# A graph-attention kernel: the attention stage with segmented maxima on 56 partitions, PSUM operands for VectorE, and an unrolled order

## What is computed

```
feat_src = (feat @ W_n).reshape(N, H, D)
el, er = einsum('nhd,hdt->nht', feat_src, attn_l / attn_r);  em = einsum('ef,hft->eht', e_pro, attn_m)
e = (einsum(el[src], mask) + einsum(er[dst], mask) + einsum(em, mask)) / 3.0
e = where(e > 0, e, NEG_SLOPE * e)
e_max = segment_max(e, dst)
e_exp = exp(e - e_max[dst])
a = e_exp / segment_sum(e_exp, dst)[dst]
rst = segment_sum(feat_src[src] * a[:, :, None], dst)
...
x = x + attention(relu(layernorm(x)));  x = x + layers(relu(layernorm(x)))
```

## Time and profile before

| what | us |
|---|---|
| median of 3 runs | 4303.44 |
| lowest, highest | 4292.51, 4304.95 |
| the profiled execution, its own time | 4305.03 |
| its span in the profile | 4301.5 |
| gathers of the attention stage: first start | 155.1 |
| last weighing of rows (L1506) starts | 1680.7 |

### The profile page before, as it was taken

One profiled execution on the slowest core, in us unless ns is written; L12 is line 12 of the kernel. 1 busy time (PEld: TensorE's weight loads), 2 busy tenths in 40 slices (PEclk: granted clock), 3 DMA queues, 4 the chain that ended last, 5 costly groups with the idle time before them and its releaser, 6 DMA issues.

```text
span 4301.5 us, 47883 instructions
## 1 busy us (share of the span) xinstructions
PE 3329.9 (77%) x13132; PEld 2370.4 (55%) x13132; DVE 2106.5 (49%) x5235; ACT 1030.1 (24%) x2694; POOL 3076.5 (72%) x2940
## 2 busy tenths in 40 slices
PE   4378888777877777888888868888887687878765
PEld 3266666555555564555666545565665455555554
DVE  4588888666666676222332422233333223344354
ACT  2134444333333343111111210111112111111111
POOL 0368878687878784777777757777777577777775
PEclk9678888777677788999999988999999889999987
DMA  4367777544444454665666436666664366666653
GB/s 150 106 176 217 220 217 222 167 131 133 130 134 135 133 162 120 196 192 185 190 188 193 141 117 193 185 197 189 195 186 138 112 201 193 197 197 210 190 147 111
DMA packets 441679, 730.92 MB, mean 170 GB/s; under 512 B 113602, under 2 KB 290894, under 8 KB 441390
## 3 DMA queue, kind: packets, MB, share of 16 engines
q0 software_dynamic: 139888, 388.79, 32.5%
q1 hardware_dynamic: 299436, 336.87, 24.3%
q10 hardware_dynamic: 2066, 1.93, 0.1%
HBM read 608.13 MB, written 119.14 MB: 169 GB/s over the span
## 4 chain that ended last, share of the span: by engine, by line
POOL 37%; issue 12%; PE 8%; DMA 3%; DVE 0%; ACT 0%; SPq 0%; POOLq 0%; DVEq 0%
POOL ring L457 37%; PE ps L1176 4%; PE ps L1124 2%; DMA block_sums<-message_sums 1%; DMA ring<-message_table,src_index 1%; PE ps L1160 1%; PE ps L1153 1%; PE ps L1193 1%; DMA message_sums<-sums_out 0%; PE ps L585 0%; DMA message_table<-block_msg 0%; DVE block_cube L691 0%; DVE block_inv_norm L693 0%; SPq L1055 0%; DVE block_o L1230 0%
## 5 line engine op out<-in xcount | busy, mean ns | idle before, releaser
L457 POOL DMA_INDIRECT ring<-message_table,src_index x1995 | 1888.1, 946 | 716.0 <-issue 603.8
L1176 PE MATMUL ps<-ring,one_hot 128*128 128x256 f32 x3990 | 1089.2, 426 | 361.3 <-DMA ring<-message_table,src_index 354.0
L457 POOL DMA_INDIRECT ring<-attention_table,src_index x784 | 1023.2, 1305 | 294.0 <-issue 236.8
L1176 PEld LDWEIGHTS ps<-ring,one_hot 128*128 128x128 f32 x3990 | 829.2, 214 | 651.2 <-DMA ring<-message_table,src_index 467.4
L1230 DVE SCALAR_TENSOR_TENSOR block_o<-ps,inv_deg,root 128x256 f32<-128x256 f32 x147 | 71.0, 483 | 1013.1 <-PE ps L1153 1013.0
L1124 PE MATMUL ps<-attention_work 128*128 128x512 f32 x1176 | 550.8, 600 | 20.3 <-DMA attention_work<-message_table 20.3
L521 PE MATMUL ps<-ring,one_hot 128*128 128x265 f32 x1568 | 531.2, 478 | 8.9 <-issue 7.5
L521 PEld LDWEIGHTS ps<-ring,one_hot 128*128 128x128 f32 x1568 | 337.8, 233 | 96.2 <-issue 33.0
L1124 PEld LDWEIGHTS ps<-attention_work 128*128 128x128 f32 x1176 | 226.7, 193 | 240.2 <-issue 205.0
L1210 DVE TENSOR_SCALAR shift_mat<-ps,shift_by 128x128 f32<-128x128 f32 x282 | 97.5, 346 | 490.0 <-PE ps L1193 445.9
L1273 ACT ACTIVATE sums_out<-ps 128x256 f32<-128x256 f32 x285 | 109.1, 383 | 865.6 <-PE ps L1193 810.7
(11 more groups left out here) (157 smaller groups left out, 3666.3 us busy)
## 6 DMA issues: line engine op xcount, KB each, us to landing
attention_work<-dense_adjacency SPq DMA_DIRECT2D x294, 256.0 KB, 3.0
attention_work<-in_dst_edges SPq DMA_DIRECT2D x112, 448.0 KB
attention_work<-message_table SPq DMA_DIRECT2D x294, 128.0 KB, 3.6
message_sums<-sums_out SPq DMA_DIRECT2D x285, 128.0 KB, 2.2
ring<-message_table,src_index POOLq DMA_INDIRECT x1995
dense_adjacency<-root SPq DMA_DIRECT2D x49, 512.0 KB
message_table<-block_msg SPq DMA_DIRECT2D x147, 128.0 KB, 2.7
block_sums<-message_sums SPq DMA_DIRECT2D x123, 128.0 KB, 3.5
```

What stands on the lines that cost most here:

```text
L457: pool.indirect_dma_start(m.ring[:, k, t, 0:cols], None, table, bass.IndirectOffsetOnAxis(ap=m.src[:, at:at + 1], axis=0)).then_inc(s[f"ro ...
L1176: last = nc.tensor.matmul(m.ps[:, 6 + parity, 0:D], m.one_hot[:, parity, t, :], m.ring[:, k, t, 0:D], start=(t == 0), stop=(only and t == ...
```

## The change

`attention` is written anew.

- Maxima are taken inside a tile of 128 edges with a halo of 48 edges at each side (RUN goes from 40 to 48), so the 7 tiles x 8 heads lie on 56 partitions, each 224 long (REACH). A check in `setup` covers all edges and sends a graph with a run longer than that to the general path. With full maxima the running rescale (`drop`, `fall`, `carry`) is gone.
- Each large VectorE operation has one operand in PSUM: the weights that ACT writes, the forward scan, and the constants of the comparisons.
- PE adds the gathered left scores to the kinds with an identity matmul. The one-hot matrices are made by DVE with one comparison instead of by ACT.
- The inverse square root of the node step is computed on DVE.
- All engines' programs are unrolled, and the order of steps is another.

The diff, cut to its core:

```diff
-RUN = 40
+RUN = 48
+REACH = P + 2 * RUN
 @block.tensor
+            def left_of(c):
+                rows_in(pe, c)
+                nc.tensor.matmul(m.ps[:, 0, 0:TILES * 32].rearrange("p (t n) -> p t n", t=TILES), m.ident[:],
+                                 m.ring[:, c % SLOTS, :, WIDE:ROW], start=False, stop=True).then_inc(s["kinds"].sem, 1)
+            def to_heads(c):
+                if c + 1 < CHUNKS:
+                    pe.wait_ge(s["leaky"].sem, s["leaky"].done(c + 1))
...
+                nc.tensor.matmul(m.ps[0:cols, 1, RUN:RUN + P], m.score[:, at:at + cols], m.ident[:], start=True, stop=True)
...
+            def to_edges(c):
+                cols = TILES * HEADS
+                pe.wait_ge(s["bwd"].sem, s["bwd"].done(c))
+                nc.tensor.transpose(m.ps[:, 1, 512 - cols:512], m.seg_max, m.ident[0:cols, 0:cols]).then_inc(s["mt"].sem, 1)
...
+            def sum_chunk(c):
+                parity, k = c % 2, c % SLOTS
+                pe.wait_ge(s["denoms"].sem, s["denoms"].done(c))
+                pe.wait_ge(s["weighed"].sem, s["weighed"].done(c))
+                pe.wait_ge(s["onehot"].sem, s["onehot"].done(c))
...
+            for c in range(CHUNKS):
+                if c + 1 < CHUNKS:
+                    left_of(c + 1)
+                to_heads(c)
+                if c + 2 < CHUNKS:
+                    kinds_of(c + 2)
+                to_edges(c)
+                if c - 1 in slot_at:
+                    turn(slot_at[c - 1])
+                sum_chunk(c)
+                if c - 1 in slot_at:
+                    project(slot_at[c - 1])
 @block.vector
-            def step(score, weigh, total):
...
+            def run_maxima(c):
...
+                forward = m.ps[0:cols, 1, REACH:2 * REACH]
+                nc.vector.tensor_tensor_scan(forward, m.flags[:, k, 0:REACH], m.ps[0:cols, 1, 0:REACH],
+                                             -FAR, ALU.add, ALU.max).then_inc(s["fwd"].sem, 1)
...
+                nc.vector.tensor_tensor_scan(m.run_max[:, RUN:][:, ::-1], m.flags[:, k, RUN + 1:REACH + 1][:, ::-1],
+                                             forward[:, RUN:][:, ::-1], -FAR, ALU.add, ALU.max).then_inc(s["bwd"].sem, 1)
+            def weigh(c):
...
+                weights = m.weights[:, c % 2].rearrange("p (t h) -> p t h", h=HEADS)
+                nc.vector.tensor_tensor(ring_heads[k][:, :, :, 0:HD], ring_heads[k][:, :, :, 0:HD],
+                                        weights[:, :, :, None].to_broadcast([P, TILES, HEADS, HD]),
+                                        ALU.mult).then_inc(s["weighed"].sem, 1)
...
+            for c in range(CHUNKS):
+                if c + 1 < CHUNKS:
+                    score_of(c + 1)
+                if c + 2 < CHUNKS:
+                    other_side(c + 2)
+                run_maxima(c)
+                below_max(c)
+                if c + 1 < CHUNKS:
+                    compare(c + 1)
+                weigh(c)
+                if c in slot_at:
+                    node(slot_at[c])
+                if c - 2 in slot_at:
...
+                    biased(slot_at[c - 2])
 @block.scalar
+            def soften(c):
+                act.wait_ge(s["diff"].sem, s["diff"].done(c))
...
+                nc.scalar.activation(m.weights[:, c % 2], m.diff, ACT.Exp, scale=1.0 / 3.0).then_inc(s["expd"].sem, 1)
+                nc.scalar.activation(ring_heads[c % SLOTS][:, :, :, HD], m.diff.rearrange("p (t h) -> p t h", h=HEADS), ACT.Exp,
+                                     scale=1.0 / 3.0).then_inc(s["denoms"].sem, 1)
...
+        m.weights = m.ps[:, 2, 0:2 * 64].rearrange("p (k e) -> p k e", k=2)[:, :, 0:TILES * HEADS]
+        m.iota_att, m.step_att, m.window_ps = m.ps[:, 3, 0:P], m.ps[:, 3, P:2 * P], m.ps[:, 3, 2 * P:2 * P + CHUNKS]
```

516 lines of the change are left out of this document (275 added, 241 removed).

## The result

| | before | after |
|---|---|---|
| median of 4 runs, us | 4304.19 | 4526.93 |
| lowest, highest | 4292.51, 4309.67 | 4523.92, 4529.10 |
| span of the profiled execution | 4301.5 | 4527.1 |

The changed kernel is slower: ratio 1.0521, 95% interval 1.0498 to 1.0544, 223 us. The forecast was 4490 us, slower, with a range of 4240 to 4580.

A forecast was written before the change was run, and what follows sets the result against it. POOL bounded the old stage; afterwards a ring of PE and DVE waits would, 12.7 + 2.1 = 14.8 us a chunk against 13.19. That gave +179 and +7 on 4305.03: 4490 us, range 4240 to 4580.

The forecast's parts named there:

- The bound and what leaves it: Attention stage: POOL bounds the old kernel; with PSUM operands a gather falls from 1.31 to 0.95 us, 277 us less on POOL.
- rival 4: POOL's gathers: PSUM operands free nothing, gathers stay at 1.31 us, 11.3 and 15.4 us a chunk; chance counted inside the others.
- rival 2: Attention stage: POOL stays the bound, with short gathers, giving 4035 us; chance 0.04.
- The ring: Attention chunk: PE and DVE wait for each other in series, one turn 12.7 us a chunk at full clock.
- DVE idle ahead of the score: Sign in each chunk: DVE waits 4 to 6 us for the left scores' matmul where no node step stands there.
- part 3: Turning scores to heads, making kinds of c+2 and turning maxima back, on PE: 3.1 us a chunk, hiding DVE's scans.
- weighing to first sum: DVE's weighing of 1792 elements ahead of PE's sum matmuls: 1.94 us a chunk.
- The clock: PE in the attention stage: mean granted clock 0.6 to 0.75, adding 2.1 us a chunk, 14.8 us in all.
- ten of sixteen: PE's sum and shift passes taken to run at the low clock, 0.21 us more each, 2.1 us a chunk.
- rival 1: Attention stage: the ring holds but PE's clock stays full, 12.7 us a chunk, 4258 us in all; chance 0.15.
- Outside the chunks: Start of the kernel: counting repeated edges over 48 neighbours adds 4.6 and some 2 us, stores and check nothing to 1; +7.
- The node step: DVE's step per node block: lies beside 3.7 us of matmuls and the left scores, so costs some tenths at most.

The follow-up runs named there:

- Experiment 5: Weights of the big multiply moved from PSUM to SBUF: 4260.30 us with the chunk order of the open ring, 4527.23 us in the changed kernel.
- experiment 3: Changed kernel plus four throwaway matmuls of 256 columns (the fillers) on PE ahead of each chunk's sums: 4333.52 us, ratio 1.008.
- experiment 6: Changed kernel with the setup load of shifted destinations split from 127 partitions into 112 and 15: 4512.78 us, ratio 1.049.
- open ring: Changed kernel with the same operations reordered, later chunks' scores, maxima, comparison and kinds moved beside the sums of c: 4185.04 us, ratio 0.974.
- experiment 2: Changed kernel with PE making the kinds of chunk c+2 behind the turned maxima of c instead of ahead: 4438.31 us, ratio 1.034.
- divided kernel: Open ring with the split load, the node step's inverse square root moved behind the next chunk: 4777.98 us on one chip, 4143.99 us on another.
- open ring with the split load: Open ring plus the setup load split into 112 and 15 partitions: 4175.89 us, ratio 0.970; run again, 4170.95 us, ratio 0.970.

## Why the prediction was right

**The bound and what leaves it.** Right. POOL was the bound, its gathers fell to 0.95 us, which excludes rival 4, and it has waits of 478 / 96 = 5.0 us in nearly every chunk instead of 46.9 us in all, which excludes rival 2. Experiment 5 gives one large operation its second SBUF input back, and gathers of 2.3 us return.

**The ring.** Right, and it is what the experiments show most directly: three edits that change no work, only who stands ahead of whom, gave 103, 89 and 342 us. Of the signs named for it POOL's waits are there, and so is PE idle ahead of the sums, 361.8 / 107 = 3.4 us (3 to 4 named); PE also waits 1.23 us ahead of the turned scores in the turn shown (1.3 named). DVE idle ahead of the score is there, but longer than named: "4 to 6 us where no node step stands there" is 8.0 us in the 46 chunks with a projection and 6.0 in the other 15. The mean of 545.0 / 108 = 5.0 us takes in the chunks with a node step, 1.8 us each.

**Its length.** 15.06 against 14.8 us. The mis-sized term is **part 3**, 3.39 us in the mean against 3.1. It is 2.99 in the turns without a projection, as forecast, and 3.92 in those with one. There the kinds take 3.05 us instead of 2.21, since the granted clock over them is 0.76 in the mean instead of 1.00. The text had put the kinds at a mixed level into the range and not into the sum. The other parts are each within 0.2 us, and here some luck comes in: weighing to first sum and left scores are 0.27 us over, sums, difference and comparison 0.25 under, and the two cancel.

**The clock.** The mean was 0.74, inside 0.6 to 0.75. Of fourteen sum passes 9.3 ran low and of the two shift passes none, close to the ten of sixteen of the sum. The ten was a choice, though: the 3.2 us of rows 7 that it leans on are 7 passes of 0.44. That the term is real and of this size is shown by experiment 3: with the clock of the sums nearly restored the chunk is 1.58 us shorter. Without the term the forecast would have been rival 1's 4258, faster than before, and the sign would have been wrong. The kernel with the fillers took 4334 and not 4258 because its chunk is 13.5 us and not 12.7: against the forecast part 3 is 0.3 us longer, the left scores and the way from weighing to first sum 0.24 each, the sums 0.16, and the start adds 9.5 us.

**Outside the chunks.** Wrong in size: +16.5 us against +7, out of two errors of opposite sign. The step that failed is "Two more stores and a larger check at the start ... are nothing to 1 us": it doesn't name the load of 127 partitions, to which experiment 6 gives 13.3 us of the first weighing's 16.5 and 14 us of the time, by its shape and not its size. The other step counted 4.6 us and some 2 for 48 neighbours. Here is the longer reduction after, where the earlier trace rows has 11.6 us:

```profile
L492 DVE TENSOR_REDUCE root<-root 128x140 f32<-128x6720 f32 x1 | 12.3, 12300 | 0.0
```

A fifth more elements took 0.7 us more, its twin went from 10.9 to 11.7, and the comparison from 7.6 to 9.5: 3.4 us in all, which is about what remains beside the load, 16.5 - 13.3 = 3.2.

**The node step.** "Costs some tenths at most" holds in the changed kernel, where its 4.4 us lie beside 5.7 us of sums. In the open ring it doesn't: 0.41 us a chunk came from moving half of it. A cover is a property of the order, and goes with it.

**The sum.** 111 x 1.87 + 16.5 = 224 measured, 111 x 1.61 + 7 = 186 forecast. Of the 38 us between them 29 are the chunks (part 3 alone would be 111 x 0.29 = 32), and 9.5 the start: 13.3 of the load, less 3.8 by which the count and the rest were put too high.

## What to carry to other kernels

When a change rewrites the order of in-order engines, follow one value through both engines from one chunk to the next before counting what each engine saves: if every large operation of a chunk stands on that path, the savings of each are lost in waits, and no engine's share shows it. A saving on the engine that was the bound should be priced in the new order (the same PSUM operand was worth some 70 us in one and nothing in the other). Here the waits on PE came with a low clock in the matmuls behind them, and that cost more than any one term of the ring; filling such a wait raised that clock in experiment 3 and not in experiment 2, so it has to be tried. A transfer whose number of partitions changed is looked at even when it stands far from the stage that was rewritten: 127 partitions cost 14 us here.

## What the runs showed of the hardware

- Work ahead of a run of matmuls didn't by itself bring the full clock. With fourteen passes of 32 columns and two of 224 ahead of them, the sums of one chunk ran at a granted clock of 0.50 although PE had been busy since 1000.67 us (experiment 2; 10.4 of 14 low in the mean); with eight passes of 256 columns ahead and a gap of 1.61 us they ran at 1.00 (experiment 3; 1.2 of 14 low in the mean). What in the work makes the difference these runs don't settle.
- A load of the same table took 12.09 us to issue on 127 partitions, and 1.45 us as 112 and 15. In the first case six loads of another queue took 2.6 to 3.4 us each to issue, in the second none over 1.0.
- A weighing with its small operand in PSUM takes 2.01 us, as with both in SBUF (2.02); only the gathers beside it notice, 0.95 against 1.10 us in the mean.
- On one chip of the study the kernel before took 4781 us, against 4295 to 4304 on the others. In the layers of the divided kernel there the gathers took the usual 0.95 us, with longer waits around them. Its ratio was 0.999 there and 0.963 on another chip, so this ratio didn't carry over; between two of the other chips the open ring with the split load had 0.970 both times.
